# A Mamba, attention and expert stack: the decay product of sixteen chunks on GpSimd, and a new instruction order

## The reference

```python
x = x + 0.5 * lora_ffn(layernorm(x))      # 8 experts of rank 16, softmax gate, base 128x128
x = x + mamba2(layernorm(x))              # 4 heads of 64, state 128, conv 4, in 2 batches of 2048
x = x + 0.5 * lora_ffn(layernorm(x))
x = x + 0.5 * moe(layernorm(x))           # top 2 of 8 experts of 176, and a shared expert of 352
x = x + linear_attention(layernorm(x))    # 16 heads of 8; context summed over each batch
x = x + 0.5 * moe(layernorm(x))
# in mamba2, per token, the chunked form of
h = h * exp(dt * A) + dt * x[..., None] * B ;  y = einsum('bhpn,bn->bhp', h, C)
```

## Time and profile before

| | us |
|---|---|
| median of 3 executions | 946.68 |
| lowest and highest | 939.96 and 947.03 |
| the profiled execution, its own time | 947.6 |
| its span, first to last instruction | 946.3 |
| TensorE busy in it | 827.4 |

### The profile page before, as it was taken

How to read it: one execution, slowest core, us unless ns; L and a number is a source line. 1 busy time by engine, 2 the same in 40 slices (tenths; PEclk the granted TensorE clock), 3 DMA queues, 4 the chain that set the end, 5 groups by cost and what they waited for, 6 DMA issues and landing times.

```text
span 946.3 us, 15952 instructions
## 1 busy us (share of the span) xinstructions
PE 827.4 (87%) x4890; PEld 635.9 (67%) x4890; DVE 556.3 (59%) x1900; ACT 572.7 (61%) x1335; POOL 529.2 (56%) x648
## 2 busy tenths in 40 slices
PE   7999999999999987999789878987997895995983
PEld 6668688587776676686666667756666662764762
DVE  5487687877475757578546455598773461461113
ACT  4899787479877776786356335753743552552451
POOL 4058252586345787166753656565475665555453
PEclk9999998999999999999899899998997996998997
DMA  9920000010100012001131113121111421321323
GB/s 301 413 97 1 1 1 2 32 49 13 29 24 12 30 49 82 12 23 35 55 105 39 45 46 113 45 82 55 51 43 43 131 65 56 91 82 47 102 69 115
DMA packets 55652, 63.50 MB, mean 67 GB/s; under 512 B 7483, under 2 KB 47419, under 8 KB 55355
## 3 DMA queue, kind: packets, MB, share of 16 engines
q1 hardware_dynamic: 45299, 41.21, 14.2%
q0 software_dynamic: 9984, 20.60, 6.7%
q10 hardware_dynamic: 288, 0.67, 0.2%
HBM read 27.53 MB, written 34.92 MB: 66 GB/s over the span
## 4 chain that ended last, share of the span: by engine, by line
PE 48%; issue 14%; DVE 11%; POOL 11%; ACT 7%; DMA 6%; another core or an unknown queue 3%; SPq 0%; POOLq 0%; DVEq 0%; ACTq 0%
PE psum L529 8%; PE psum L800 7%; PE psum L820 6%; POOL sorted_x L1718 5%; PE psum L609 4%; PE psum L749 3%; PE psum L734 3%; PE psum L739 3%; DMA sent_y<-e_y,e_sx 2%; POOL sent_y L1728 2%; DMA e_sx<-sorted_x 2%; PE psum L678 2%; PE psum L842 2%; PE psum L524 1%
## 5 line engine op out<-in xcount | busy, mean ns | idle before, releaser
L1728 POOL DMA_INDIRECT sent_y<-e_y,e_sx x184 | 182.9, 994 | 156.1 <-ACT e_y L1557 111.4
L1718 POOL DMA_INDIRECT sorted_x<-g_xn,r_slot x128 | 129.0, 1008 | 38.6 <-issue 32.8
L800 PE MATMUL psum<-gu_w,e_sx 128*128 x368 | 129.4, 479 | 5.6 <-issue 3.5
L1252 DVE TENSOR_TENSOR e_h<-e_h,psum 128x352 f32<-128x352 f32 x96 | 47.8, 502 | 140.7 <-ACT e_h L1549 94.1
L820 PE MATMUL psum<-d_w,e_h 88*128 x736 | 104.5, 288 | 17.8 <-issue 13.7
L820 PEld LDWEIGHTS psum<-d_w,e_h 88*128 88x128 f32 x736 | 95.3, 200 | 34.8 <-issue 33.4
L1557 ACT ACTIVATE e_y<-psum,e_sx 128x128 f32<-128x128 f32 x184 | 57.5, 362 | 96.6 <-PE psum L820 57.2
L800 PEld LDWEIGHTS psum<-gu_w,e_sx 128*128 128x128 f32 x368 | 65.8, 197 | 34.9 <-issue 15.4
L1375 ACT ACTIVATE e_h<-psum 88x512 f32<-88x512 f32 x96 | 54.5, 572 | 48.0 <-PE psum L529 29.7
L1549 ACT ACTIVATE e_h<-psum 128x352 f32<-128x352 f32 x96 | 42.8, 450 | 62.5 <-PE psum L800 40.9
L529 PE MATMUL psum<-w_ffn,e_h 128*88 128x128 f32 x368 | 58.1, 283 | 20.8 <-issue 12.0
(11 more groups left out here) (241 smaller groups left out, 1933.0 us busy)
## 6 DMA issues: line engine op xcount, KB each, us to landing
e_sx<-sorted_x SPq DMA_DIRECT2D x88, 130.0 KB
sorted_x<-c_ys SPq DMA_DIRECT2D x8, 975.0 KB, 20.2
c_ys<-sent_y SPq DMA_DIRECT2D x14, 512.0 KB
sorted_x<-c_ys SPq DMA_DIRECT2D x8, 520.0 KB, 19.9
sent_y<-e_y,e_sx POOLq DMA_INDIRECT x184
xs<-in_x SPq DMA_DIRECT2D x8, 256.0 KB, 7.5
sorted_x<-g_xn,r_slot POOLq DMA_INDIRECT x128
out<-xs SPq DMA_DIRECT2D x7, 256.0 KB
```

Source lines behind the costliest of these rows:

```text
L800: last = e.matmul(two.banks[j].tile[:, 0:2 * IEXP], e_xT[k % SXS][:, j, :], gu_w[:, bass.ds(which[j] * (2 * IEXP), 2 * IEXP)], start=True, ...
L1718: e.indirect_dma_start(out=sorted_x[g], out_offset=bass.IndirectOffsetOnAxis(ap=r_slot[n][:, k, t:t + 1], axis=0), in_=rows[:, j, :], in_o ...
L1728: e.indirect_dma_start(out=sent_y[g], out_offset=bass.IndirectOffsetOnAxis(ap=e_sx[k % SXS][:, j, DM:DM + 1].bitcast(U32), axis=0), in_=e_ ...
```

## The change

Three things are changed. The product of `m_et` and `gm` of the first batch's sixteen chunks (k under `MASKED` = 16) moves from VectorE to GpSimd, with a semaphore of its own, `m_Mp`; the instruction has the same operands. Thirteen lengths of pieces are set to other values, eight lower (by 0.05 to 0.87 us) and five higher, and pieces on VectorE and ScalarE free their engine 0.1 us earlier in the plan (`NEXT`). All rank tables but `GAP`, `TAP_STEP` and `FOLD_AT` have new numbers. No other instruction's operation or shape changes; only the count of fill matmuls follows from the plan.

```diff
-FIRST = [177.82, 370.46, -25.93, -76.55, -165.11, 314.87, 71.46, 191.43]
+FIRST = [-1715.61, 1914.27, 664.92, 952.17, -1196.83, -8.41, 120.13, 1071.38]
...
+MASKED = 16
...
-LATENCY, PE_LATENCY, TRANSFER, TABLE = 0.12, 0.25, 2.2, 1.3
+LATENCY, PE_LATENCY, TRANSFER, TABLE, NEXT = 0.12, 0.25, 2.2, 1.3, 0.1
...
-        free[name] = begin + course.cost
+        signals.now = begin + course.cost
+        free[name] = signals.now - (NEXT if name in ("vector", "scalar") else 0.0)
...
+        def masked(k):
+
+            return ("m_Mp", k + 1) if k < MASKED else ("m_M", k + 1 - MASKED)
...
-                yield (t + 4.5, 1.26, ("bank", 1), ("m_M", k + 1), ("m_xdt", k + 1),
+                yield (t + 4.5, 1.26, ("bank", 1), masked(k), ("m_xdt", k + 1),
...
-                on.wait_ge("m_M", k + 1)
+                on.wait_ge(*masked(k))
...
-                yield t + 2.5, 0.82, ("m_decay", k + 1), ("m_gm", k + 1)
-                on.wait_ge("m_decay", k + 1)
-                on.wait_ge("m_gm", k + 1)
-                e.tensor_tensor(et[:, :, :], et[:, :, :], gm.unsqueeze(1).broadcast_to([P, HEADS, P]),
-                                ALU.mult).then_inc(*S.up("m_M"))
+                if k >= MASKED:
+                    yield t + 2.5, 0.7, ("m_decay", k + 1), ("m_gm", k + 1)
...
+                if k < MASKED:
+                    yield t + 2.5, 1.2, ("m_decay", k + 1), ("m_gm", k + 1)
+                    on.wait_ge("m_decay", k + 1)
+                    on.wait_ge("m_gm", k + 1)
+                    e.tensor_tensor(et[:, :, :], et[:, :, :], gm.unsqueeze(1).broadcast_to([P, HEADS, P]),
+                                    ALU.mult).then_inc(*S.up("m_Mp"))
...
-                yield T + 15.0 + TAP_STEP * n, 2.5, ("m_conv", k), ("m_tap", k + 1), ("m_halo_in", k + 1)
+                yield T + 15.0 + TAP_STEP * n, 2.34, ("m_conv", k), ("m_tap", k + 1), ("m_halo_in", k + 1)
...
-                yield T + 5.5, 1.28, ("two", 1), ("e_down", k - 1), ("w_late", 16 * 3), ("e_xT", k + 1)
+                yield T + 5.5, 1.21, ("two", 1), ("e_down", k - 1), ("w_late", 16 * 3), ("e_xT", k + 1)
```

More of the change, by code:

```diff
@@ L87 @@
 ATANH = [2.0 / (2 * k + 1) for k in range(8)]
-FIRST = [177.82, 370.46, -25.93, -76.55, -165.11, 314.87, 71.46, 191.43]
-AGAIN = [135.09, -90.43, 35.89, -371.33, 70.69, 179.13, 111.78, 168.67]
-MAMBA = [-220.03, -96.33, 78.29, 264.38, -151.98, 471.11, 141.78, 20.16]
-CHUNK_AT = [24.78, 17.98, 107.37, 30.64, 119.59, 76.35, 60.04, 58.75]
+FIRST = [-1715.61, 1914.27, 664.92, 952.17, -1196.83, -8.41, 120.13, 1071.38]
+AGAIN = [910.43, -724.42, 738.25, -2328.53, -30.14, 394.29, 992.28, 107.49]
+MAMBA = [-898.41, -197.62, 635.19, -572.84, -971.23, 600.34, 184.67, -1534.13]
+CHUNK_AT = [465.66, -207.4, 404.51, -92.24, -780.73, -281.63, -103.06, -1989.37]
+MASKED = 16
 GAP = 4.9
@@ L97 @@
 FOLD_AT = 35.0
[L98 to L106, removed]
+FINISH = [-694.88, -94.03, 864.92, 388.09, -1495.27, 144.2, -550.4, 65.5]
+GATED = [-1032.44, -740.01, -2123.26, -598.95, 137.65, 1345.49, 553.1, 108.48, -653.4, 1366.2, 667.66, -103.06, -630.9, -312.55, -114.1, -302.04]
+SORTED = [-192.71, -174.54, 803.52, -209.39, 135.68, -844.23, -1364.75, 1408.88]
+PAIRED = [91.96, 1317.02, -127.52, -268.26, 1793.62, -196.55, 1081.15, 2450.33]
+PACE = [23.94, 55.05, -13.04, 51.14, 2.04, 77.34, 153.96, -28.38]
+SENDS = [461.69, 806.19, 1614.41, -228.61, 1123.42, 1514.45, 660.8, 1497.03]
+COMBINED = [-1225.7, 1582.19, -981.8, 2001.19, 2008.5, 1536.69, 989.1, 2267.89, 608.53, -1160.37, 979.82, -322.43, 1744.33, 2781.91, -1648.5, 51.17]
+KV = [1769.45, 2302.92, -503.14, 377.35, 1309.8, -490.07, 683.4, 412.1]
+SECOND = [-472.59, -12.58, 877.79, -120.82, 1019.9, 1248.57, -57.04, 855.77]
 TAPPED_BY = [sum(len(TAPPED[k // BLK_PER_BATCH]) for k in range(b)) for b in range(NBLK + 1)]
@@ L277, in weave @@
             signals.late, free[name] = PE_LATENCY, clock.run(begin, course.cost)
-        signals.now = free[name]
+            signals.now = free[name]
         if not course.go_on():
@@ L981, in mamba @@
                 row = lambda k: dtt[:, k, :]
-                yield T, 1.8, ("f0_res", FFN0_AT[0, b] + 1), ("m_sum", b - 1)
+                yield T, 1.56, ("f0_res", FFN0_AT[0, b] + 1), ("m_sum", b - 1)
                 mv, veps, rstd, shifted, grown = m_ln_parts(m_ln[s])
@@ L1071, in chunk @@
                                     ALU.add).then_inc(*S.up("m_state"))
-                yield t + 6.0, 1.27, ("m_Y", k + 1), ("m_dx", k + 1)
+                yield t + 6.0, 1.22, ("m_Y", k + 1), ("m_dx", k + 1)
                 ybank = banks.tile("m_Y", k)
@@ L1651, in chunk @@
                 ch = m_ch[k % CHUNKS]
+                et, gm = m_et[k % 2], ch[:, 3 * P:4 * P]
                 xh = heads(ch[:, 0:DINNER])
@@ L1674, in finish @@
                 T, rs = FINISH[b], m_rs[b % 2]
-                yield T + 0.5, 1.29, ("m_sq", 4 * b + 4), ("m_res", b - 1)
+                yield T + 0.5, 1.6, ("m_sq", 4 * b + 4), ("m_res", b - 1)
                 on.wait_ge("m_sq", 4 * b + 4)
@@ L1700, in scatter @@
                     for half in range(2):
-                        yield (T + 8.0 + 4.0 * nth + 2.0 * half, 2.5, ("r_slot", g + 1), ("g_xn", i + 1), ("zeros", 16 * sum(EMPTY_LOADS)),
+                        yield (T + 8.0 + 4.0 * nth + 2.0 * half, 2.5 if half else 3.1, ("r_slot", g + 1), ("g_xn", i + 1), ("zeros", 16 * sum(EMPTY_LOADS)),
                                ("w_gates", 16), ("g_score", i + 1), *before)
@@ L1740, in attn_out @@
                 T, s, x = SECOND[b], b % 2, blk(b)
-                yield T, 1.23, ("k_q", b + 1), ("w_late", 16 * 3)
+                yield T, 1.38, ("k_q", b + 1), ("w_late", 16 * 3)
                 on.wait_ge("k_q", b + 1)
@@ L1832, in experts @@
                 before = stored(k - 2) if k >= SXS else ("const", 1)
-                yield PAIR[g][t], 0.0, *scattered(g), before
+                yield PAIR[g][t], 0.45, *scattered(g), before
                 for signal in scattered(g):
```

11 lines of the change are left out of this document (6 added, 5 removed).

## The result

The change made the kernel slower, by less than 2% but clear of the noise: 953.34 us in the median (948.42 to 963.87, 20 runs) against 939.90 for the kernel before in the same measurement (931.86 to 951.22, 20 runs), a ratio of 1.0158 (95% interval 1.0136 to 1.0181). The forecast had said 935 us against the three-run median of 946.68, a ratio of 0.988. The profiled execution took 956.0 us, its span is 954.7. Lines of the file have moved: L524 is now L530, L529 L535, L734 L740, L749 L755, L820 L826, L1060 L1067, L1557 L1564, L1718 L1732, L1728 L1742; the product on GpSimd is L1673.

What follows compares the result with a forecast made beforehand. TensorE's work plus what it waits or fills was taken as the bound. Terms of -1.5, +1, -6.3, -2, 0 and -3 summed to -11.8 us, giving 935 us, 1.2% faster; the range was 916 to 956.

Steps and rivals of the forecast that it cites:

- Term 1: VectorE, first batch's scan: losing 16 products, mostly beside other engines' work, gains little; -1.5 us, bounds 0 and -11.3.
- Term 2: GpSimd, first batch's scan: 16 more products lengthen its bursts, mostly covered by other TensorE work; +1 us, bounds 0 and +12.8.
- Term 3: Group 6 scatters, 770 to 800 us: spreading paired e_y copies removes two TensorE waits; -6.3 us, bounds 0 and -15.0.
- Rival A: Scatter bursts: ScalarE's remote waits are late transfers and stay; 943 us, no change that can be told; chance 0.24.
- Term 4: Group 3 scatters, 528 to 551 us: part of 7.5 us idle goes; -2 us, bounds -7.5 and +2; other bursts 0.
- Term 5: Outside the bursts: new ranks and trace-nearer lengths mean less fill and foreseen waiting; -3 us, bounds -14 to +14.
- B: First batch's scan: GpSimd becomes the bound, first sort and scatters start later; 953 us, slower; chance 0.13.
- C: Whole order: a new order is a new draw and meets waits the plan doesn't know; 960 us; chance 0.08.
- D: Everywhere: better lengths help, half the bursts' 44.1 us idle goes, term 5 is -8; 916 us; chance 0.16.

Runs made afterwards that it cites:

- run 1: Kernel before with its order, banks and fill replayed, only the 16 products moved to GpSimd: 944.7 us against 938.85, ratio 1.0066.
- run 2: Changed kernel with its order, banks and fill replayed, only the 16 products put back on VectorE: 956.76 us, 1.0211 of the kernel before.
- run 13: The changed kernel, unchanged, measured again on a faster chip: 900.73 us against 899.19 for the kernel before, ratio 1.001.
- run 5: Kernel before's ranks with the changed kernel's lengths and earlier engine release in the plan, products on VectorE: 1052.14 us, 1.1082 of the kernel before.
- run 7: Kernel before with its rank-table numbers randomly moved by at most 5, lengths and products as before: 1018.26 us, 1.0675 of the kernel before.

## Why the prediction was wrong

**Term 1 (-1.5)** was in kind right, but VectorE's busy time fell by 9.8 us where 11 to 13 were forecast, and by less where the order was kept: 6.1 us in run 1 (550.2 against 556.3) and 3.6 from run 2 to after (550.1 and 546.5), since its other work got longer. What that is worth by itself no run shows.

**Term 2 (+1)** was mis-sized. The product costs what the nearest row said, on tile `m_et`:

```profile
L1673 POOL TENSOR_TENSOR m_et<-m_et,m_ch x16: 1265/1277/1710, 62.6 to 176.8; 128x512 f32<-128x512 f32 x16
L1067 DVE TENSOR_TENSOR m_et<-m_et,m_ch x16: 679/688/4066, 210.8 to 443.6; 128x512 f32<-128x512 f32 x16
```

In the old order the move alone costs 0.66%, some 6 us, near the 6.4 by which I had said that one burst of eight chunks must get longer, and then called covered. In the new order, which spreads the chunks, it was covered: the products back on VectorE gave 1.0211, no better than after. Those two ratios come from different measurements, so the 0.5% between them isn't shown.

The forecast read rows 11 as stretching, "not in being a whole instruction". The longest VectorE product of the rows above says more. It began at 417.45 us, while GpSimd ran six instructions in a row, the last of them this one:

```profile
417.45 4.07 DVE L1067 TENSOR_TENSOR m_et<-m_et,m_ch 128x512 f32<-128x512 f32 x1
```

```profile
420.36 0.60 POOL L1668 TENSOR_TENSOR m_ch<-m_ch,w_scan 128x256 f32<-128x256 f32 x1
```

It ended at 421.52, 0.56 us behind GpSimd's last, and took 4.06 us at the same place in run 13. The exclusive port lock of the Trainium skill (SBUF — State Buffer, "SBUF: two separate sides"), by which the sum would have been 1.5 us higher, agrees with this row. As a bound on what it takes from VectorE, 20.4 us was far too high: of the 11.3 us that 16 products at 0.708 are, 5.2 us came back as longer work in run 1 and 7.7 between run 2 and after, one profiled execution each. GpSimd's own 32 products of `m_ch` by `m_dt` got cheaper when VectorE's products no longer stood beside them, 682 to 627 ns from run 2 to after and 674 to 652 in run 1:

```profile
L1665 POOL TENSOR_TENSOR m_ch<-m_ch,m_dt 128x256 f32<-128x256 f32 x32 | 20.1, 627 | 7.0 <-ACT m_ch L1382 6.3 <-DVE m_ch L1062 0.6
```

**Term 3 (-6.3)** failed by its mechanism, though the idle time of its stretch came near. I took TensorE's waits of 4.08 and 2.24 us for waits on ScalarE's copies standing together, and spread copies for their cure. The copies were waiting for TensorE, whose own down projection signalled late, and the row after shows them spread and 7.92 us late. That 770 to 800 holds 4.4 us less idle time all the same (8.0 against 12.4, where "under 7" and a clock above 0.85 were to show the step right), and the eight bursts 12.0 us less where terms 3 and 4 had said 8.3, isn't shown to come from the spread copies; as far as the runs tell, it is luck. The forecast had named the open question (it "doesn't say which of the two was late") and then priced only one side. Rival A's "against" held the other in half a line ("TensorE's part in these waits is as open").

**Term 4 (-2)**: the burst of group 3 holds 7.5 us idle after as before (14.48 busy of 22). 0.

**Term 5 (-3)** is the step that failed by size, and it turned the sign. Idle time outside the bursts was to be at or under 75 us and is 83.0; fill was to be near 59 and is 61.7; and the term had no place for TensorE's busy time, which rose by 12.2 us with less fill. "The new lengths are nearer to this trace, so the plan should be off by less" isn't borne out: in run 5, with the ranks of before, they made the kernel 10.8% slower. The 14 us by which I bounded a new draw came from a tenth of idle and fill time; two shaken orders cost 6.75 and 6.77%, some 60 us. Against draws of that width, -11.8 us from local differences was no forecast of a sign.

**The rivals.** A's sign, waits of 3 to 8 us there again, came true, but neither its time (no change) nor its reason, late transfers, did. B's sign came without its mechanism: group 0 began 20 us later, and it was made up. C's mechanism, a new draw, is what the runs support, and its time is the nearest (960 us on a base of 946.7 is 1.014); it has stops of over 3 us on TensorE at new places, 6.74 us at 784 and 6.0 at 814. D fell.

**What stays open.** On the first chip after is 1.6% slower, on another 0.1% (run 13), and the halts are not simply more: 37.1 against 41.3 us in the two profiled runs. TensorE was busy for 67.6 us at half clock before and for 85.2 after; at full clock this work would take half of that, so the slow clock cost some 33.8 and 42.6 us. The difference would cover the 8.4 us between the two spans, but one profiled run each is thin, and the clock may be what follows. Over the unprofiled runs of a kernel, a clock lower by 0.01 goes with 4 to 8 us in most measurements. Why the halts come, and what they have to do with the clock that falls behind them, no run here tells, nor why after loses on the chips that have them. That no trace of two chips has any, that they stand mostly near scatters after 450 us, and that four large ones of after came again in run 2 at the same places does stand.

## What to carry to other kernels

Where an order comes from tuned numbers, a "trace-true" length or a shifted rank is another draw: freeze the old order, try the edit in it, and forecast the new order with the spread of shaken ones (here two, 7% slower both), not from the places that look better. A wait that a profile puts down to something remote is to be tested on instructions that need only one engine; if those wait too, it is that engine, however finished its rows look. And a difference of 1 to 2% should be run on a second chip before it is called the kernel's.

## What the runs showed of the hardware

- The chips differ by up to 6% for the same program: before took 938.85, 940.41 and 953.08 us on three, 898.29 and 899.19 on two others. On the latter, no trace has a halt of TensorE; on the former, and in the traces of before and after, each has 9 to 17.
- TensorE's idle stretch in a halt reached 12.7 us (at 491 us in run 7). The one shown began at a granted clock of 1.00, and half clock stood behind it (0.50 in 790.5 to 796); why is not shown.
- With more fill the clock of the profiled runs was higher: 0.918 (none), 0.949 (211), 0.963 (383), in three measurements. Of the three counts, 211 was the fastest, by 0.6% over none and 2.5% over 383.
- A GpSimd product of 128x512 from two SBUF tiles took 1.277 us in the median and at most 1.71; VectorE's took 0.688 in the median, and 4.07 where it met six GpSimd instructions in a row.
